# Feed-forward down products of two token groups: from float32 to three float32r passes

## The reference, cut to what matters

```
h   = layernorm(x)                                  # tokens x 256
mlp = silu(h @ gate_w) * (h @ up_w) @ down_w        # 256 -> 1024 -> 256
ew  = silu(h . down_embed[indices]) * softmax(scores)
experts_states = sum_k ew_k * up_embed[indices_k]   # 512 experts of one hidden unit each
x   = x + tanh(g_ffn[0]) * (mlp + experts_states)
```

## Time and profile before

| what | value |
|---|---|
| median of three runs | 510.68 us (510.35 to 511.2) |
| the profiled execution's own time | 510.63 us |
| its span, first to last instruction | 508.8 us |
| PE busy | 444.7 us (87%) |
| DVE busy | 357.5 us (70%) |
| ACT busy | 245.0 us (48%) |
| POOL busy | 156.8 us (31%) |
| mean granted TensorE clock | 0.964 |

### The profile page before, as it was taken

The page is one execution under the profiler, slowest core; times in us unless marked ns, Lnnn a source line. Parts: engine busy times, 40 slices in busy tenths (PEclk is TensorE's granted clock), DMA queues, the critical chain, the costliest instruction groups (busy, mean ns, idle before and its releaser), DMA issues. The chain is left out here.

```text
span 508.8 us, 7205 instructions
## 1 busy us (share of the span) xinstructions
PE 444.7 (87%) x2130; PEld 353.8 (70%) x2130; DVE 357.5 (70%) x1026; ACT 245.0 (48%) x453; POOL 156.8 (31%) x157
## 2 busy tenths in 40 slices
PE   1517999599999999999999999898998899899990
PEld 1315678467678877888778787787776688788860
DVE  6996669998577986585987967978778454621173
ACT  3608666355295355337044417270651644955540
POOL 3965324240002221100000000050426015477771
PEclk9965999799999999999999999999999999999996
DMA  8510222000200001950000000132323323346394
GB/s 299 199 32 16 63 88 64 21 1 0 96 9 0 2 0 57 308 145 0 2 0 1 1 1 1 32 102 76 120 87 101 108 81 114 104 145 196 107 386 138
DMA packets 32965, 42.00 MB, mean 83 GB/s; under 512 B 3483, under 2 KB 26781, under 8 KB 32928
## 3 DMA queue, kind: packets, MB, share of 16 engines
q1 hardware_dynamic: 28224, 32.28, 21.3%
q0 software_dynamic: 3744, 8.42, 4.5%
q10 hardware_dynamic: 960, 0.86, 0.5%
HBM read 24.97 MB, written 18.39 MB: 85 GB/s over the span
## 5 line engine op out<-in xcount | busy, mean ns | idle before, releaser
L666 PE MATMUL acc<-w_down,act_s 128*128 128x256 f32 x384 | 90.8, 383 | 0.9 <-DVE act_s L1406 0.9
L666 PEld LDWEIGHTS acc<-w_down,act_s 128*128 128x128 f32 x384 | 73.6, 192 | 12.6 <-DVE act_s L1406 1.3
L642 PE MATMUL ring<-xt_h,up_l 128*128 128x512 f32 x160 | 70.5, 440 | 2.9 <-DVE xt_l L1376 1.5
L1621 POOL TENSOR_TENSOR rstd<-var_eps,minus_half 128x4 f32<-128x4 f32 x14 | 14.9, 1067 | 171.4 <-DVE var_eps L1205 171.4
L644 PE MATMUL ring<-xt_h,up_h 128*128 128x512 f32 x160 | 64.1, 401 | 0.0
L643 PE MATMUL ring<-xt_l,up_h 128*128 128x512 f32 x160 | 64.1, 401 | 0.0
L1117 ACT ACTIVATE act_s<-ring 128x512 f32<-128x512 f32 x48 | 28.6, 596 | 69.1 <-PE ring L644 68.9
L705 PE MATMUL ring<-up_e,act_s 128*128 x184 | 44.2, 382 | 2.3 <-issue 2.1
L1660 POOL DMA_INDIRECT x_rows<-main_a,slots x32 | 31.0, 970 | 43.7 <-ACT main_a L1138 34.8
L637 PE MATMUL ring<-small,xn 128*128 128x128 f32 x144 | 21.7, 300 | 25.5 <-ACT xn L1009 13.3
L1410 DVE TENSOR_TENSOR act_s<-ring,act_s 128x512 f32<-128x512 f32 x32 | 22.0, 686 | 30.4 <-PE ring L644 19.0
(11 more groups left out here) (277 smaller groups left out, 978.0 us busy)
## 6 DMA issues: line engine op xcount, KB each, us to landing
main_b<-x_rows SPq DMA_DIRECT2D x22, 257.0 KB, 3.0
x_rows<-v_t SPq DMA_DIRECT2D x1, 3983.5 KB, 16.0
up_l<-y_rows SPq DMA_DIRECT2D x5, 512.0 KB, 6.4
stage<-in_w_mlp SPq DMA_DIRECT2D x8, 256.0 KB, 2.6
up_e<-in_w_moe SPq DMA_DIRECT2D x8, 256.0 KB, 2.6
x_rows<-v_t SPq DMA_DIRECT2D x1, 1927.5 KB, 22.2
x_nat<-in_x SPq DMA_DIRECT2D x7, 256.0 KB, 7.5
out_x<-x_nat SPq DMA_DIRECT2D x6, 256.0 KB, 5.6
```

The source lines that it names most:

```text
L642: pe.matmul(out, wl, xh, start=first, stop=False, skip_group_check=True)
L666: last = pe.matmul(acc[t // 2][:, t % 2, :], act_s[n % RING][:, tok], w_down[:, u, :], start=u == 0 and t % 2 == 0, stop=final, skip_group ...
```

## The change

For f = 2 and f = 3 (SPLIT_DOWNS) each down product becomes three float32r products into the same bank: high hidden by low weights, high hidden by high weights, low hidden by high weights. The parts are made on chip.

- Hidden values: a new step ("hidden", f, u) stands right after ("mlp", f, u + 2). ACT copies act_s to a high part act_h (two buffers, in the place of v_t). Then POOL (f = 2) or DVE (f = 3) subtracts, and the low part act_l takes the place of act_s.
- Weights: a new step ("weights", 2, u), two in each of the parts 2 to 7 of f = 2. ACT copies a weight block to the place of the low part, POOL turns that into the low part, and ACT then rounds w_down in place to the high part. The low parts of the first eight blocks lie in main_b, those of the last four in v_odd.
- SP waits before the first load of rows into main_b until the eight MLP units of f = 3 are done.

```diff
+SPLIT_DOWNS = (2, 3)
     for part in range(1, MLP_UNITS + 2):
         SCHED.append(("mlp", f, part))
...
+        if f in SPLIT_DOWNS and 2 <= part < MLP_UNITS + 2:
+            SCHED.append(("hidden", f, part - 2))
         if part in PLAN[("mlp", f)]:
...
     ("mlp", 2): {
-        2: "attn_in 0 1, query 3 1, route 2 2",
-        3: "attn_in 0 2, route 2 3 4",
-        4: "attn 0 0 1 2 3, route 2 5",
+        2: "attn_in 0 1, query 3 1, route 2 2, weights 2 0 1",
+        3: "attn_in 0 2, route 2 3 4, weights 2 2 3",
+        4: "attn 0 0 1 2 3, route 2 5, weights 2 4 5",
...
@@ PE, down(f, u)
+                if f in SPLIT_DOWNS:
+                    pe.wait_ge(act_low, split_turn(f, u) + 1)
+                    if f == SPLIT_DOWNS[0]:
+                        pe.wait_ge(down_high, u + 1)
+                    for t in range(GT):
+                        tok = slice(t * P, (t + 1) * P)
+                        out = acc[t // 2][:, t % 2, :]
+                        pe.matmul(out, act_h[:, n % 2, tok], low_of(u), ...)
+                        pe.matmul(out, act_h[:, n % 2, tok], w_down_h[:, u, :], ...)
+                        last = pe.matmul(out, act_l[:, n % RING, tok], w_down_h[:, u, :], ...)
+                    last.then_inc(down_done, 1)
+                    return
@@ ACT
+                elif kind == "hidden":
+                    n = unit_of(g, part)
+                    hidden_made(act, n)
+                    if split_turn(g, part) == 0:
+                        act.wait_ge(rows_cleared, 32)
+                    if split_turn(g, part) >= 2:
+                        act.wait_ge(down_done, n - 1)
+                    act.activation(act_h[:, n % 2, :], act_s[n % RING][:, :], ACT.Copy).then_inc(act_high, 1)
+                elif kind == "weights":
+                    u = part
+                    act.wait_ge(down_done, unit_of(g - 1, u) + 1)
+                    if u == 0:
+                        full(act, (("query", NG - 1), "Q"))
+                    act.activation(low_of(u), w_down[:, u, :], ACT.Copy).then_inc(down_rounded, 1)
+                    for w in (u - 1, u) if u == MLP_UNITS - 1 else (u - 1,) if u > 0 else ():
+                        act.wait_ge(down_low, w + 1)
+                        act.activation(w_down_h[:, w, :], w_down[:, w, :], ACT.Copy).then_inc(down_high, 1)
@@ DVE
+                elif kind == "hidden" and g == NG - 1:
+                    n = unit_of(g, part)
+                    dve.wait_ge(act_high, split_turn(g, part) + 1)
+                    dve.tensor_tensor(act_l[:, n % RING, :], act_s[n % RING][:, :], act_h[:, n % 2, :].bitcast(F32),
+                                      ALU.subtract).then_inc(act_low, 1)
@@ POOL
+                elif kind == "hidden" and g < NG - 1:
+                    n = unit_of(g, part)
+                    pool.wait_ge(act_high, split_turn(g, part) + 1)
+                    pool.tensor_tensor(act_l[:, n % RING, :], act_s[n % RING][:, :], act_h[:, n % 2, :].bitcast(F32),
+                                       ALU.subtract).then_inc(act_low, 1)
+                elif kind == "weights":
+                    u = part
+                    pool.wait_ge(down_rounded, u + 1)
+                    pool.tensor_tensor(low_of(u), w_down[:, u, :], low_of(u).bitcast(F32), ALU.subtract).then_inc(down_low, 1)
@@ SP, load_pair
+                if n == 0:
+                    sp.wait_ge(down_done, unit_of(NG - 1, IC - 1) + 1)
```

More of the change, by code:

```diff
@@ L332, in build @@
         minus_mean = sb("minus_mean", [P, 2, GT])
+        with nc.sbuf_tensor("act_h", [P, 2, GN], F32R) as act_h:
+            pass
         v_t = [sb(f"v_t{c}", [P, GN]) for c in range(C)]
+        with nc.sbuf_tensor("w_down_l_late", [P, MLP_UNITS - IC, D], F32R) as w_down_l_late:
+            pass
         v_odd = [sb(f"v_odd{c}", [P, GN]) for c in range(C)]
         main_a = [sb(f"main_a{c}", [P, 2, GT * PAD]) for c in range(C)]
+        with nc.sbuf_tensor("w_down_l", [P, IC, D], F32R) as w_down_l:
+            pass
         main_b_words = sb("main_b", [P, C * 2 * GT * PAD])
@@ L360, in build @@
         xt_f = xt_f_pad[:, 0:C * GN].rearrange("p (c n) -> p c n", c=C)
+        with nc.sbuf_tensor("act_l", [P, RING, GN], F32R) as act_l:
+            pass
         act_s = [sb(f"act_s{k}", [P, GN]) for k in range(RING)]
@@ L406, in build @@
         up_e = sb("up_e", [P, UPS])
+        with nc.sbuf_tensor("w_down_h", [P, MLP_UNITS, D], F32R) as w_down_h:
+            pass
         w_down = sb("w_down", [P, MLP_UNITS, D])
@@ L472, in build @@
         down_done = sem("down_done")
+        act_high = sem("act_high")
+        act_low = sem("act_low")
+        down_rounded = sem("down_rounded")
+        down_low = sem("down_low")
+        down_high = sem("down_high")
         acc_free = sem("acc_free")
@@ L567, in hidden_made, with split_turn, low_of @@
                 freed(eng, ((kind, f), "B", u))
+        def split_turn(f, u):
+            return SPLIT_DOWNS.index(f) * MLP_UNITS + u
+        def low_of(u):
+            return w_down_l[:, u, :] if u < IC else w_down_l_late[:, u - IC, :]
         def sent(eng, grp):
@@ L661, in down @@
                     pe.wait_ge(acc_free, 2 * f)
+                final = u == MLP_UNITS - 1
+                if f in SPLIT_DOWNS:
[5 more added lines that the diff above has]
+                        out = acc[t // 2][:, t % 2, :]
+                        pe.matmul(out, act_h[:, n % 2, tok], low_of(u), start=u == 0 and t % 2 == 0, stop=False,
+                                  skip_group_check=True)
+                        pe.matmul(out, act_h[:, n % 2, tok], w_down_h[:, u, :], start=False, stop=False,
+                                  skip_group_check=True)
+                        last = pe.matmul(out, act_l[:, n % RING, tok], w_down_h[:, u, :], start=False, stop=final,
+                                         skip_group_check=True)
+                    last.then_inc(down_done, 1)
+                    return
                 hidden_made(pe, n)
-                final = u == MLP_UNITS - 1
                 for t in range(GT):
```

## The result

The changed kernel takes 530.51 us, the median of four runs (530.03 to 532.04), beside 510.94 us (510.35 to 511.7) for the kernel before on the same chip: a ratio of 1.0381, 95% interval 1.0362 to 1.0399. That is 19.6 us slower, where 11.5 were forecast; the time lies 2.5 us above the range. The direction was right, and the size was not.

The account below looks back on a forecast made before the run. PE was taken to bound 210 to 389 us, with DVE and ACT's bank releases limiting close behind. Terms 8.7 - 1.5 + 3.6 - 0.7 + 1.4 = +11.5 on 510.63 gave 522 us; 8-in-10 range 514.5 to 528.

Parts of the forecast that it names:

- head, to the output product of f = 2: Start of f = 2: ACT waits for clearing DMAs, added copies and POOL waits follow; 8.7 us lost, ends 6.5 and 10.5.
- rest of f = 2, to the first up product of f = 3: Eight or nine PE-bound units save 0.264 us each, with little DVE slack; 1.5 us gained (0 to 3.5).
- f = 3, to its output product: DVE sets the pace; five subtractions of 0.72 us precede the output product's operand; 3.6 us lost (1.5 to 5).
- from there to the last unit of f = 3: From 348 us, four units save 1.0 us on PE and DVE's waits absorb its subtractions; 0.7 us gained.
- exit: End of f = 3: later copies, row sends and last down product, side by side; 1.4 us lost (0.5 to 3).
- PE's part: Down products on PE: 256-column float32r instructions 0.122 us apart, saving 0.264 us a unit, 6.3 us over 24 units.
- 216 ns for 512 columns: The skill's issue-gap figure for PE, which the forecast said float32 rows meet and float32r rows miss by 17 ns.
- The wait until 223.1: Head of f = 2: ACT stands still 5.9 us, from 217.2 until the later zeroing DMA lands at 223.1.
- "So its work is hidden, except where ACT waits for it": POOL's 23.8 us of subtractions in f = 2 cost nothing except ACT's waits, as POOL does little else there.
- 10.5 as an end: Upper end of the head's 8.7 us loss, if DVE slows POOL's subtractions.
- The clock: Rival: PE's idle times in the head bring one or two half-clock stretches costing 2 to 4 us, up to 526; chance 0.10.
- 3.35 us of idle time in 47: PE's idle time from 301 to 348 us before the change, at clock 1.00; argued against the clock falling.

Follow-up runs that it names:

- the second experiment: Only PE's float32r down products, on ready operands, without the copies, subtractions and weight steps of the changed kernel: 510.37 us, ratio 0.9982 to the kernel before.
- three causes out: Changed kernel with tiles exchanged (no clearing-DMA wait for hidden copies), no DVE subtractions in f = 3, POOL's subtractions on 8 columns: 516.35 us, ratio 1.0085.
- the three causes and the exit out: Changed kernel without clearing-DMA wait or f = 3 DVE subtractions, POOL's on 8 columns, f = 3 units 10 and 11 as single float32 products: 511.45 us.

## Why the forecast was right on the direction and too small

By its own steps, in lateness of the profiled execution:

| step | forecast | measured |
|---|---|---|
| head, to the output product of f = 2 | 8.7 | 10.4 |
| rest of f = 2, to the first up product of f = 3 | -1.5 | +1.6 |
| f = 3, to its output product | 3.6 | 3.4 |
| from there to the last unit of f = 3 | -0.7 | +1.3 |
| exit | 1.4 | 2.7 |
| sum | 11.5 | 19.4 |

- **PE's part** held: 0.118 us an instruction (0.122 forecast), 0.315 a unit. (The float32 rows with which the forecast compared its 216 ns for 512 columns have 256 columns, so they don't bear that figure out; no term of the sum rests on it.) That it is worth nothing in the head and little elsewhere held too; the second experiment gives 2.4 us of the 7.5 by the end of f = 3.
- **The wait until 223.1** held (it ended at 223.8), with the chain behind it: silu of unit 3 at 237.70 (237.1 forecast), silu of unit 4 at 247.24 (246.5), unit 5 on PE at 247.88 (247.1).
- **"So its work is hidden, except where ACT waits for it"** is the step that failed. POOL had time enough, but a subtraction on POOL slows a DVE operation that meets it: 0.69 became 1.66 us ahead of the output product, and seven such rows sum to 4.05 us more DVE time in f = 2. Of the 1.7 us by which the head came out larger than forecast, 1.0 is that one operation, and 0.7 is the clearing DMA's later landing. The forecast counted only the other way round (10.5 as an end, "if POOL's subtractions are slowed by DVE"). Removing POOL's work gave back 5.5 us. The Trainium skill's page "SBUF — State Buffer" (who interferes with whom) has the rule: a DVE instruction with both inputs in SBUF and a GpSimd one that reads SBUF exclude each other, and whichever starts second stands still until the first is done. The trace agrees roughly: the DVE operation starts 0.35 us behind POOL's and takes 0.97 us more, of POOL's remaining 1.10.
- **The clock** was a rival at 0.10, with one or two stretches for 2 to 4 us, and is part of the outcome in its place: four stretches near 261, 333, 363 and 401. The forecast argued that 3.35 us of idle time in 47 had left the clock at 1.00; that was a sum over a long stretch, and says nothing on how the idle time lies in it; the rows here show PE busy 0.6 to 1.0 us of the 3 us ahead of each fall. The rest of f = 2 comes out at +1.6 instead of -1.5 and this is put down to the stretch at 261 (1.7 us) and DVE's slowed operations; the step from the output product of f = 3 on at +1.3 instead of -0.7 by that at 363. The Trainium skill's warning on gaps between bursts ("TensorE: Matmul & The Clock Gate", HAM oscillation) was weighed and left to that rival. The trace agrees that idle time between bursts can bring the half clock, but not every such gap did: the one of 2.50 us before 238.35, in the head where the forecast looked for it, left the clock at 1.00.
- **f = 3's subtractions** held (3.6 and 3.4 us), though the measured figure has a half-clock stretch in it (332.7), so the agreement in size is partly luck.
- **The exit** was 1.4 with an upper end of 3, and measured 2.7. The missed part is order on DVE: unit 10's low part waits behind unit 11's mask operations, which the forecast took for ready when its copy is. PE's wait of 3.83 us then halves the clock for the last two units.

What isn't settled: how the clock's part divides. Each cause taken out alone also takes away or moves stretches, and one pair of runs shows it falling and not falling behind the same gap. The exit's worth is shown only with the other three causes out. The sum is nearly settled: with the three causes and the exit out, 0.6 of the 19.6 us is left by the medians, and 1.2 (0.1 to 2.3) by the ratio.

## What to carry to other kernels

Work put on an idle POOL is not free if DVE is near the critical path: look at which DVE operations it will meet, and price them at up to the remaining length of POOL's instruction. Where PE is nearly full but paced by others, look for each new wait at the idle time close around it, not at its share of the stage, and put the half clock behind it into the range: it may come or not. And before pricing what parts cost, run the best case of the gain by itself: here it was 0.9 us where PE's own time fell by 7.5, which nearly settles the change before any of its costs. And run the kernel that one compares with on each chip that is used: a DMA that landed 1.5 to 2.6 us later on the second chip took from two experiments what they were made to show.

## What the runs showed of the hardware

- float32r products with 256 columns follow at 0.116 to 0.118 us, half of the 0.233 with 512, and at 0.213 on the 1.2 GHz clock.
- The clock fell right behind idle times of PE of 1.98 us (332.33), 2.24 (363.58), 2.42 (260.62) and 3.83 us (402.79) in the changed kernel, and of 2.40 us in the kernel with three causes out, where one of 1.47 us in its place left it full. The length of one gap doesn't decide it: 2.50 us before 238.35 in the changed kernel and 2.92 us before 272.65 with units 10 and 11 as before left it at 1.00, and 2.35 us at the same point of two runs brought both outcomes.
- With PE's part alone and nothing added to any engine, the clock fell at 393.0, in an idle time of 1.24 us of PE ahead of its first product on the loaded rows, which it did not in the kernel before.
- The same DMA of 1927.5 KB landed 21.7 to 22.9 us after its issue in nine profiles, and 24.3 to 25.4 in the four from a second chip.
